# A deformable-convolution layer on one core: the sampling stage's loop over strips, its coarse patch buffer and the order of its start

## The reference

```python
fine = group_norm(x)
coarse_up = resize(coarse, (B, 64, 64, 256), 'bilinear')
attn = sigmoid(mean(fine, axis=(1, 2)) @ attend_w)
fine_cal = (fine * (attn + 1)) @ select_w
align = concat([fine_cal, coarse_up * 2], -1) @ offset_w
om = conv3x3_same(align, om_w, om_b)          # 216 channels
off, mask = om[..., :144], sigmoid(om[..., 144:])
# 8 groups x 9 taps: each tap reads coarse_up at a shifted, fractional place
# (four neighbours, bilinear weights, zero outside), times its mask
val = gather_bilinear(coarse_up, y + ky + off_y, x + kx + off_x) * mask
out = x + relu(einsum('bhwkc,kcf->bhwf', val, dcn_w) + dcn_b) + fine_cal
```

## Time and profile before

| what | value |
|---|---|
| median of 3 runs | 3216.22 us (3210.22 to 3219.1) |
| profiled execution, its own time | 3217.3 us |
| its span in the profile | 3215.5 us |
| granted TensorE clock, mean | 0.971 |
| TensorE busy (matmul) | 3030.1 us, 94% |
| VectorE busy | 2518.1 us, 78% |
| ScalarE busy | 1519.0 us, 47% |
| GpSimd busy | 335.7 us, 10% |

### The profile page before, as it was taken

How to read it: one execution, slowest core, us unless ns; L and a number is a source line. 1 busy time by engine, 2 the same in 40 slices (tenths; PEclk the granted TensorE clock), 3 DMA queues, 4 the chain that set the end, 5 groups by cost and what they waited for, 6 DMA issues and landing times.

```text
span 3215.5 us, 90885 instructions
## 1 busy us (share of the span) xinstructions
PE 3030.1 (94%) x33906; PEld 2633.8 (82%) x33906; DVE 2518.1 (78%) x4299; ACT 1519.0 (47%) x2787; POOL 335.7 (10%) x445
## 2 busy tenths in 40 slices
PE   7799999999999828999998999998999998999999
PEld 7689999989999826888887888887888887888887
DVE  5448888878888849888886888887888886888881
ACT  0122222222222116666665666665666665666662
POOL 2000000000000001111111111111111111111110
PEclk9889999999999959999999999999999999999999
DMA  6333244324434232233223232223223223222221
GB/s 212 103 109 64 54 69 64 60 43 64 60 51 50 31 62 45 56 65 63 54 62 60 61 58 62 62 55 69 54 62 66 54 61 61 61 55 65 62 60 50
DMA packets 452627, 207.13 MB, mean 64 GB/s; under 512 B 230820, under 2 KB 447540, under 8 KB 452276
## 3 DMA queue, kind: packets, MB, share of 16 engines
q1 hardware_dynamic: 426112, 161.74, 28.6%
q10 hardware_dynamic: 21724, 26.37, 2.5%
q0 software_dynamic: 4608, 16.78, 1.4%
HBM read 104.86 MB, written 55.23 MB: 50 GB/s over the span
## 4 chain that ended last, share of the span: by engine, by line
PE 52%; ACT 6%; issue 3%; DVE 1%; ACTq 1%; SPq 1%; DMA 0%; POOL 0%; POOLq 0%; DVEq 0%
PE eb L1556 29%; PE tb L1114 15%; PE vb L1136 6%; ACT taps_all L1085 2%; ACT res L1143 2%; ACT wtT L1119 1%; ACT om L1041 1%; PE eb L1149 1%; PE tb L1036 1%; ACT mask L1050 1%; ACTq L1007 1%; DVE wt L1108 0%; SPq L1031 0%; DMA rt<-r_d 0%; DMA om_s<-om_d 0%
## 5 line engine op out<-in xcount | busy, mean ns | idle before, releaser
L1556 PE MATMUL eb<-val,wd 128*128 128x256 f32 (+1 forms) x4680 | 1219.1, 384 | 0.0
L1119 ACT COPY wtT<-tb 128x512 f32<-128x512 f32 x1152 | 663.6, 588 | 607.8 <-PE tb L1114 606.3
L1556 PEld LDWEIGHTS eb<-val,wd 128*128 128x128 f32 x4680 | 794.6, 190 | 121.2 <-issue 57.3
L1108 DVE TENSOR_TENSOR wt<-taps_all 128x768 f32<-128x768 f32 x768 | 731.7, 994 | 10.4 <-PE tb L1114 2.1
L1114 PE MATMUL tb<-ident,wt 128*128 128x128 f32 x4608 | 700.2, 275 | 34.6 <-ACT wtT L1119 18.8
L1114 PEld LDWEIGHTS tb<-ident,wt 128*128 128x128 f32 x4608 | 560.8, 141 | 178.2 <-ACT wtT L1119 59.3
L548 PE MATMUL conv<-fine,wf 128*108 128x256 f32 x4608 | 593.1, 289 | 14.5 <-DVE omT L879 14.5
L548 PEld LDWEIGHTS conv<-fine,wf 128*108 128x108 f32 x4608 | 572.4, 173 | 30.5 <-issue 30.5
L1136 PE MATMUL vb<-wtT,win 64*32 64x144 f32 x16384 | 318.4, 289 | 39.7 <-issue 33.3
L1489 DVE COPY val<-vb 128x432 f32<-128x432 f32 (+1 forms) x384 | 212.7, 554 | 143.4 <-PE vb L1136 143.0
L1136 PEld LDWEIGHTS vb<-wtT,win 64*32 64x32 f32 x16384 | 241.9, 106 | 83.3 <-issue 83.3
(11 more groups left out here) (138 smaller groups left out, 2320.7 us busy)
## 6 DMA issues: line engine op xcount, KB each, us to landing
val<-val SPq DMA_DIRECT2D x128, 396.0 KB, 3.8
win<-cpad SPq DMA_DIRECT2D x304, 64.0 KB
om_s<-om_d SPq DMA_DIRECT2D x1152, 12.0 KB
chunk<-in_x SPq DMA_DIRECT2D x32, 512.0 KB, 6.0
xchunk<-in_x SPq DMA_DIRECT2D x32, 512.0 KB, 3.9
r_d<-r POOLq DMA_DIRECT2D x32, 512.0 KB, 3.2
rt<-r_d SPq DMA_DIRECT2D x63, 256.0 KB, 4.9
out<-ot ACTq DMA_DIRECT2D x63, 256.0 KB, 2.2
```

Of the source, the lines that this page charges most:

```text
L1108: return nc.vector.tensor_tensor(wt[b][:, PER * d:PER * (d + 1), WQ * u:WQ * (u + 1)].rearrange("p k (a b) -> p k a b", a=WIN), of_rows(0) ...
L1119: return nc.scalar.copy(dst, src) if e == "act" else nc.vector.tensor_copy(dst, src)
L1556: done = nc.tensor.matmul(eb[q][:, 256 * fo:256 * fo + rows], wd[:, half, k, 128 * fo:128 * fo + 128], val[:, half, k, at:at + rows // W, ...
```

## The change

It touches the sampling stage alone.

1. `loop` writes all strips out on TensorE, ScalarE and VectorE; no hardware loop is left on these three. TensorE's sampling waits compare with constants, and its `to_reg` and the wait on `consts` beside them go from `first_runs`.
2. A second patch buffer: image b uses `wins[b % 2]`. All 16 window transfers of image b + 1 are issued in one go (`whole_windows`), before strips 12 to 15 of image b, with no wait in their middle. Their only wait is that image b - 1 has been sampled.
3. Constants are loaded from ScalarE's queue. SyncE issues half 0 of strip 0's offsets, ScalarE half 1, and the `wd` transfers come behind these. The first image's 16 windows stand where the first strip's were, behind the offsets of strip 2.
4. VectorE's start: strip 0's first half is capped and multiplied before `locate` 1, and its second half capped before `locate` 1; ScalarE keeps strip 1's offsets after the `taps` of strip 0.

```diff
-        win_all = sb("win", [128, 2 * BLK * 128])
-        win = win_all[:].rearrange("p (j c) -> p j c", c=128)
+        win_both = [sb(f"win{i}", [128, 2 * BLK * 128]) for i in range(2)]
+        wins = [t[:].rearrange("p (j c) -> p j c", c=128) for t in win_both]
+        win_all, win = win_both[0], wins[0]
...
-        def load_offsets(e, s, shifted, signal):
+        def load_offsets(e, s, shifted, signal, halves=range(2)):
...
-                for hx in range(2):
+                for hx in halves:
...
             def loop(e, strips):
 
-                strips(0)
-                strips(1)
-                with e.Fori(2, ST // 2 - 1) as it:
-                    strips(it)
-                for it in range(ST // 2 - 1, ST // 2 + 2):
+                for it in range(ST // 2 + 2):
                     strips(it)
...
+                def whole_windows(b):
+
+                    w(sp, "sampled", 6 * SI * (b - 1))
+                    windows(b, b * (PADC * PADC * C), range(WIN), sems["win_whole"])
...
                     w(sp, "sampled", 6 * s)
-                    if turn is None:
-                        windows(at, range(2, WIN), sems["win_first"])
-                        h(sp, "win_first", 16 * 12 * (b + 1))
-                        windows(at, range(0, 2), sems["win_ready"])
-                    else:
-                        at = at + 2 * (i - turn) * (PADC * C)
+                    if turn is not None:
+                        at = b * (PADC * PADC * C) + 2 * (i - turn) * (PADC * C)
                         if not isinstance(at, int):
                             at = sp.snap(at)
-                        windows(at, range(2 * turn + 6, 2 * turn + 8), sems["win_ready"])
+                        windows(b, at, range(2 * turn + 6, 2 * turn + 8), sems["win_ready"])
...
-                load_offsets(sp, 0, True, sems["om_loaded"])
+                load_offsets(sp, 0, True, sems["om_loaded"], (0,))
...
-                opening(0)
-                with sp.Fori(1, 4) as m:
-                    four(0, 4 * m)
-                with sp.Fori(1, B - 1) as b:
+                whole_windows(0)
+                for b in range(B):
                     opening(b)
-                    with sp.Fori(1, 4) as m:
+                    with sp.Fori(1, 3) as m:
                         four(b, 4 * m)
-                opening(B - 1)
-                with sp.Fori(1, 3) as m:
-                    four(B - 1, 4 * m)
-                four(B - 1, 12)
+                    if b + 1 < B:
+                        whole_windows(b + 1)
+                    four(b, 12)
...
-                for s in range(2):
-                    keep(s, s, s)
+                load_offsets(act, 0, True, sems["om_loaded"], (1,))
+                load_weights(act)
+                act.wait_ge(consts, CONSTS)
+                keep(0, 0, 0)
                 for hx in range(2):
                     taps(0, 0, hx)
+                keep(1, 1, 1)
...
                     measure(0, 0, hx)
+                cap(0, 0, 0)
+                products(0, 0, 0)
+                for d in range(3):
+                    third(0, 0, 0, d)
+                cap(0, 0, 1)
                 dve.wait_ge(sems["dist_ready"], 4)
                 locate(1, 1)
                 dve.wait_ge(sems["pchain"], 2 * NPOS)
                 measure(1, 1, 0)
-                for hx in range(2):
-                    cap(0, 0, hx)
-                products(0, 0, 0)
-                for d in range(3):
-                    third(0, 0, 0, d)
...
-                        copied, loaded, kept = (v if isinstance(v, int) else pe.to_reg(v) for v in (
-                            batch_no(s, hx, NT - 1) + 1, 64 * (s + 1), 3 * n))
-                        pe.wait_ge(consts, CONSTS)
-                        w(pe, "tb_out", copied)
+                        w(pe, "tb_out", batch_no(s, hx, NT - 1) + 1)
                         if hx == 0:
-                            w(pe, "win_ready", loaded)
-                        w(pe, "kept_near", kept)
-                        w(pe, "kept_far", kept)
+                            w(pe, "win_whole", 16 * 16 * (s // SI + 1))
+                            w(pe, "win_ready", 64 * (s // SI * (SI - 1) + s % SI))
+                        w(pe, "kept_near", 3 * n)
+                        w(pe, "kept_far", 3 * n)
...
             @block.sync
             def _(sp):
-                load_constants(sp)
                 choose(sp, fast_sp, gen_sp)
...
             @block.scalar
             def _(act):
-                act.wait_ge(consts, CONSTS)
-                load_weights(act)
+                load_constants(act)
                 act.wait_ge(const_set, 1)
                 choose(act, fast_act, gen_act)
```

More of the change, by code:

```diff
@@ L978, in sample_and_project, with load_constants @@
         TABLES = 5
-        def load_constants(sp):
+        def load_constants(e):
             by_row = coords_d.rearrange("(j r c) n -> r j c n", j=BLK, r=4)
             for r in range(4):
-                sp.dma_start(coords[32 * r:32 * r + 32], by_row[r]).then_inc(consts, 16)
-            sp.dma_start(ident[:], ident_d).then_inc(consts, 16)
+                e.dma_start(coords[32 * r:32 * r + 32], by_row[r]).then_inc(consts, 16)
+            e.dma_start(ident[:], ident_d).then_inc(consts, 16)
             with nc.allow_non_contiguous_dma(reason="256 bias values, once"):
-                sp.dma_start(bias[:], dcn_b.rearrange("(h p) -> p h", p=128)).then_inc(consts, 16)
+                e.dma_start(bias[:], dcn_b.rearrange("(h p) -> p h", p=128)).then_inc(consts, 16)
         def keep_tables(dve):
@@ L1126, in bank_of, with sample_blocks @@
             return vb[u][v % 2][:, 0:NK * 4 * m].rearrange("p (k y x) -> p k y x", k=NK, y=4)
-        def sample_blocks(half, v, window):
+        def sample_blocks(half, v, window, win):
             for j in range(*THIRDS[v]):
@@ L1160, in fast @@
             names = ("om_loaded masked pchain coef_ready dist_ready achain capped products batched tb_out based "
-                     "win_first win_ready sampled kept_near kept_far cleared sides entered crossed ready projected finished "
+                     "win_whole win_ready sampled kept_near kept_far cleared sides entered crossed ready projected finished "
                      "r_ready summed turned ob_out out_stored duplicated").split()
@@ L1221, in duplicate_rows, with windows @@
                                      ).then_inc(sems["duplicated"], 16)
-                def windows(at, rows, signal):
+                def windows(b, at, rows, signal):
                     for a in rows:
@@ L1228, in windows @@
                                           ap=[[C, WIN], [2 * C, 2 * BLK], [1, 128]])
-                            sp.dma_start(win[part:part + WIN], src).then_inc(signal, 16)
+                            sp.dma_start(wins[b % 2][part:part + WIN], src).then_inc(signal, 16)
+                def whole_windows(b):
+                    w(sp, "sampled", 6 * SI * (b - 1))
+                    windows(b, b * (PADC * PADC * C), range(WIN), sems["win_whole"])
                 def strip(b, i, turn):
@@ L1569, in first_runs @@
                         n = 2 * s + hx
[L1570 to L1573 removed]
+                        w(pe, "tb_out", batch_no(s, hx, NT - 1) + 1)
                         if hx == 0:
[L1575 to L1577 removed]
+                            w(pe, "win_whole", 16 * 16 * (s // SI + 1))
+                            w(pe, "win_ready", 64 * (s // SI * (SI - 1) + s % SI))
+                        w(pe, "kept_near", 3 * n)
+                        w(pe, "kept_far", 3 * n)
                         for v in range(2):
[L1579 removed]
+                            sample_blocks(hx, v, lambda j: BLK * hx + j, wins[s // SI % 2]).then_inc(sems["sampled"], 1)
                 def third_run(s, p, hx):
@@ L1588, in third_run @@
                         w(pe, "kept_far", one)
-                        sample_blocks(hx, 2, lambda j: BLK * hx + j).then_inc(sems["sampled"], 1)
+                        sample_blocks(hx, 2, lambda j: BLK * hx + j, wins[s // SI % 2]).then_inc(sems["sampled"], 1)
                 def slot(t, p, hx):
@@ L1736, in pe_general @@
                                     hold(pe, sems["added"], 6 * t + 2)
-                                sample_blocks(0, v, lambda j: 0).then_inc(sems["sampled"], 1)
+                                sample_blocks(0, v, lambda j: 0, win).then_inc(sems["sampled"], 1)
                             w(pe, "added", 6 * (t + 1))
```

2 lines of the change are left out of this document (removed).

## The result

The changed kernel takes 3170.53 us (median of 4 runs, 3168.95 to 3176.49) against 3213.3 us (4 runs, 3210.22 to 3219.1): a ratio of 0.9868, interval 0.9847 to 0.989. It is faster by 42 us; the prediction said 45, and 3171.5 us.

The account below looks back on a forecast made before the run. TensorE was taken to bound the kernel, with time to win only where its 30.37 us beat breaks. From 3217.3 us, -37.9 + 1.0 + 2.9 - 10.8 = -44.8 gave 3172.5, stated as 3171.5 us for the runs' median; range 3162 to 3185.

Parts of the forecast that it names:

- The crossings: Three changes of image: the second patch buffer wins all their excess over the 30.37 us beat, 37.9 us.
- The burst: 16 windows issued at once make strip 12's own windows land late at each crossing: 1.0 us lost in all.
- signs of being wrong: Idle time at crossings, a beat over 30.5 us in mid-image, or `om_s` landing over 3 us behind its last issue.
- my fourth rival: Loop back edges cost something no gap shows, so writing out gains at most 13.9 us: 3155 us; chance 4%.
- Strips written out: 58 strips go from loop to written-out form at 0.05 us more each: +2.9 us.
- The third rival: Sustained fetching of written-out code stalls, deciding from 0.82 us a strip; at 1 us a strip 3227 us; chance 5%.
- The start: Start of the sampling stage: split offset loads win 7.7 us and VectorE's new order 3.1, together 10.8 us.
- Strip 0's turn: Stage start: with offsets issued from two queues and `wd` behind them, strip 0 is turned 7.7 us earlier, at least 3.8.
- VectorE's idle time before `cap`: Stage start: 1.0 us plus a 0.2 handover stay idle of 4.28 us, so 3.1 us are won.
- the other case: First image's 16 windows take 18.6 us instead of 16.5, losing 1.9 us before the first sampling; forecast took 0.
- the second rival: The start gives only the issue time and the windows come late: 3177 us; chance 13%.
- The sum: Whole kernel: -37.9 + 1.0 + 2.9 - 10.8 = -44.8 us against the profiled 3217.3 us; forecast 3171.5 us.

Follow-up runs that it names:

- e3: The changed kernel with the old start, so only written-out strips and the second patch buffer; 3181.54 us, 0.9899 against the kernel before.
- e1: The kernel before with only the strips written out on TensorE, ScalarE and VectorE; 3217.92 us, 1.0013 against the kernel before.
- e4: The changed kernel run again unchanged, for a second profile; 3174.14 us, 0.9874 against the kernel before.
- e7: The changed kernel with the first image's 16 windows issued directly behind strip 0's offsets; 3173.74 us, 0.9864 against the kernel before.
- e6: The changed kernel with the next image's windows issued four at a time behind strips 8 to 11; 3168.5 us, 0.9856 against the kernel before.
- e10: e6 with the first image's windows issued between the offsets of strips 1 and 2; 3163.88 us, 0.9848 against the kernel before.
- e11: e10 with the `wd` transfers behind strip 0's `taps` and TensorE's wait for them at its first projection; 3169.25 us, 0.9867 against the kernel before.
- e12: e6 run again unchanged, for a second profile; 3168.93 us, 0.9863 against the kernel before.
- e8: The changed kernel with 28 more bursts of 16 windows into an unread buffer, behind strips 4 to 10 of every image; 3195.28 us in one execution.
- e5: The changed kernel with hardware loops again, one per image, on TensorE, ScalarE and VectorE; 3207.59 us, 0.9966 against the kernel before.
- e9: e6 with the old hardware loop on ScalarE and VectorE, TensorE alone written out; 3173.61 us, 0.9878 against the kernel before.

## Why the prediction was right, step by step

**The crossings: right, in mechanism and size.** Predicted 37.9 us; the chain shows 38.0, with all three crossings at 30.42 us and no wait before the samplings there. e3 against e1, 36.4 us for a predicted 36.9, says the same by the times.

**The burst: too small a term, and in the changed kernel by another wait than the named one.** I put 1.0 us on strip 12's own windows landing late, and nothing on late code. In the first profile none of the three bursts made a sampling late. In the others some did: e4 had waits of 4.30 and 2.11 us, e7 one of 3.06, e3 one of 0.84, each before the first sampling of a strip 12 of an image. The excess in the beats was 7.9, 10.6, 8.9 and 8.5 us in the changed kernel, e4, e3 and e7. In the changed kernel it is TensorE standing with its data there and the slower clock behind that, and in e3 and e7 this is the longest stall; in e4 the waits before samplings are. The kernels with the windows spread (e6, e10, e11, e12) have 0.0 to 3.5 us, and e8, with more bursts, 26.5. So the bursts make the long stalls, not the written-out code by itself, and neither by itself: e5 ran its image 0 in a loop with the same burst in it, and kept 30.38 us without a stall. That the engine waits for its code rests on the packets of q8: in the changed kernel, e3, e7 and e8 TensorE stands before the same transpose, in the first three the packet comes 17 us behind the one before it instead of 9 to 11, and the engine goes on 1.7 to 1.8 us after its end in all four. So the place in the code is fixed, and what it costs hangs on when the packet comes: e4 and e6 pass it without a stop. Which instructions a packet holds, the trace doesn't say.

Two of the prediction's own signs of being wrong came: a beat of over 30.5 in the middle of an image, by late code, and `om_s` landing over 3 us behind its last issue, below.

The Trainium skill, "Runtime: NRT & Kernel Launch", § Instruction fetch mechanics, calls the cost of going on to the next block of code "mostly hidden". The trace agrees for nearly all strips without a burst, where e6 has no stall and e10 three of up to 1.1 us; the changed kernel has one of 1.87 us behind `duplicate_rows`. It disagrees inside a burst, where TensorE stood 4.02 us. The page's other rule, on taken branches, was my fourth rival: the loop of before bears it out nowhere, e1 is slower rather than faster without it, and e5's images 1 and 2 show such a stall on a loop of the same length.

**Strips written out: right.** Predicted +2.9 us; e1 gives +4 [+1, +7], and the beat is 30.42 throughout. The third rival, code that stalls for 0.82 us or more in each strip, did not come: even the changed kernel's whole excess is 0.13 us a strip.

**The start: right in its first step, too good in its sum.** Strip 0's turn was to come 7.7 us earlier and came 8.3 earlier: the landing behind the last issue took 1.65 us where 1.72 was taken, and the issues ended 0.5 us earlier in the stage. VectorE's idle time before `cap` was to be 1.2 and is 1.18. Then the transfers were slower than the prediction had them:

- Strip 1's offsets landed 3.32 us behind their last issue, where I took 1.72: `wd` had moved from strip 0's way into theirs. e11 shows it by taking `wd` out. Strip 1's turn is 11.4 us after strip 0's, not 9.8.
- The windows took 18.2 us from their first issue to the sampling, where I took 16.5 and named 18.6 as the other case. In the seven kernels with this order it is 14.9 to 19.8 us, 17.2 in the mean, so this term was 0.7 short, and one execution can't test it.
- So TensorE waited 6.85 us for windows, and VectorE 3.90 behind it. VectorE's first copy at 1203.13 seems to meet the 1203.3 of the prediction, but only because the stage began 3.7 us earlier: in the stage's own time it is 50.3 us against 46.8 predicted. Without the 3.90 us of waiting it would be 46.4: VectorE's own chain was right.

The seven kernels with this start (after, e4, e5, e6, e8, e9, e12) have a stage start of 89.6 us in the mean (87.3 to 91.9), the three with the old one 97.7 (97.1 to 98.5). So the start gives 8.1 us in the profiles and 5 to 7 in the times, for a predicted 10.8. This is the second rival at part of its price: late windows, with strip 0's turn as early as predicted. e7 shows that windows ahead of strip 1's offsets win nothing, as these are late then. With the windows between strip 1's offsets and strip 2's (e10), TensorE doesn't wait for them, but a gain in time isn't shown.

On this the Trainium skill, "DMA: Bandwidth & Descriptors", § Issuing engines are not separate DMA queues, holds that a second issuing engine saves the time of issuing alone. By it the turn would have come 3.8 us earlier; it came 8.3 earlier, with `wd` out of the way as well, and no run here split these two.

**The sum.** -38.0 + 7.9 + 2.9 - 6.4 and -7.1 for the stage's begin and its end make the -40.7 of the spans. I had 1.0 in place of 7.9 and -10.8 in place of -6.4, 11.3 us too good, and nothing for the two outer terms, 7.1 us too bad. By the medians the kernel won 42.8 us for a predicted 44.8. The predicted time is within 1 us of the measured one partly because these errors cancel, and partly because the runs of before beside the changed kernel had a median 3 us lower than the three shown first. That it came so close is luck. The begin of the stage differs by 3.4 us between e1 and before (1153.16 and 1156.55), with the same code ahead of it, so at least that term is a matter of the execution.

## What to carry to other kernels

A transfer that is moved off the path still has to pass somewhere: look at what else uses the DMA engines in the new place, the fetch of code among it, and spread a burst over several steps where there is room (0.0 to 3.5 us of excess in place of 8 to 11). On one queue, order by when each thing is wanted; a large load put ahead of small ones makes all of them late (e7), and one taken out of one wait turns up in the next (e11). When a sum comes out right, check its terms, in time counted from a common start: here terms that were 11 us too good stood against 7 us that were not in the sum at all.

## What the runs showed of the hardware

- TensorE can stand for its code in the middle of four equal transposes: 4.02 us in the changed kernel, 3.74 in e3, 3.40 in e7 and 4.75 in e8, before the same transpose in all four. In the changed kernel the DMA engines were 0.63 to 0.76 busy there, after 16 window transfers of 64 KB. The packet of code came 17.6 us behind the one before it, and TensorE went on 1.8 us after its end. Without the burst the same code ran with no stall in 1820 us (e6), or with stalls of at most 1.1 us (e10, e11, e12).
- The 4.02 us of standing were followed by 4 us at a granted clock of 0.52 to 0.60, so that the beat grew by 5.86 us.
- A hardware loop of two strips ran without refetching in before and in e5's images 0 and 3 (4 and 6 packets of q8), and with about eight packets and 3.4 us for each iteration in e5's images 1 and 2 (58 and 60 packets). What decides it stays open.
- The beat depends on which engines run written-out code: 30.37 us with all three in a loop, 30.42 with none, 30.49 with TensorE alone written out (e9). The runs show it; why, they don't.
- 16 window transfers of 64 KB, each into 8 partitions, took 15 to 20 us from the first issue to the sampling that waits for them (seven profiles), though issued in 7.2 to 9.1.
